# The first pair of weight chunks in two loads of 256 columns each

## The reference

```python
out_nr = _gelu(x @ w1_nr + b1_nr) @ w2_nr + b2_nr                     # condition 0
out_tsr = _gelu(x @ w1_tsr + b1_tsr) @ w2_tsr + b2_tsr                # condition 1
h = _gelu(_gelu(x @ w1_sr + b1_sr) @ w2_sr + b2_sr)                   # condition 2
out_sr = h @ w3_sr + b3_sr
y = x + out
mu, var = mean(y), mean((y - mu) ** 2)
result = (y - mu) * rsqrt(var + 1e-5) * gamma + beta
```

## Time and profile before

| | |
|---|---|
| time, median of 3 runs | 558.92 us (558.64 to 558.94) |
| the profiled execution | 559.73 us |
| its span, first to last instruction | 558.0 us |
| what lies around the span | 1.7 us |
| PE busy | 548.7 us, 98% |
| DVE busy | 270.7 us, 49% |
| ACT busy | 215.6 us, 39% |
| POOL busy | 252.1 us, 45% |
| granted clock of TensorE, mean | 0.997 |

### The profile page before, as it was taken

How to read it: one execution, slowest core, us unless ns; L and a number is a source line. 1 busy time by engine, 2 the same in 40 slices (tenths; PEclk the granted TensorE clock), 3 DMA queues, 4 the chain that set the end, 5 groups by cost and what they waited for, 6 DMA issues and landing times. The chain is left out here.

```text
span 558.0 us, 8218 instructions
## 1 busy us (share of the span) xinstructions
PE 548.7 (98%) x2416; PEld 452.2 (81%) x2417; DVE 270.7 (49%) x432; ACT 215.6 (39%) x335; POOL 252.1 (45%) x212
## 2 busy tenths in 40 slices
PE   8999999999999999999999999999999999999994
PEld 5888888888888888888888888888888888888883
DVE  5650176865856856114710568112765105501656
ACT  5451236145344354214421452424255124513353
POOL 0989997775674575300430046600174300530056
PEclk9999999999999999999999999999999999999998
DMA  8984405345344443200320044400244101310032
GB/s 303 360 265 149 152 1 196 105 151 179 113 159 143 158 152 139 87 0 0 137 89 0 5 153 143 150 0 0 75 156 157 63 0 37 141 48 0 0 135 93
DMA packets 26369, 61.26 MB, mean 110 GB/s; under 512 B 3058, under 2 KB 3314, under 8 KB 26226
## 3 DMA queue, kind: packets, MB, share of 16 engines
q1 hardware_dynamic: 26208, 60.97, 31.9%
q10 hardware_dynamic: 146, 0.13, 0.1%
HBM read 44.31 MB, written 16.78 MB: 109 GB/s over the span
## 5 line engine op out<-in xcount | busy, mean ns | idle before, releaser
L489 DVE TENSOR_TENSOR g_lo<-bank,g_hi 128x512 fp32r<-128x512 f32 x112 | 77.4, 691 | 251.5 <-DVEq L121 251.5
L421 ACT ACTIVATE g_hi<-bank,bcol 128x512 fp32r<-128x512 f32 x112 | 77.8, 695 | 166.4 <-ACTq L121 165.0
L643 POOL TENSOR_TENSOR y<-y,row 128x512 f32<-128x512 f32 x64 | 96.2, 1523 | 48.2 <-POOLq L121 47.9
L459 ACT ACTIVATE y<-y,rstd 128x512 f32<-128x512 f32 x63 | 42.4, 717 | 159.8 <-ACTq L121 159.8
L248 PE MATMUL bank<-w_hi,g_hi 128*128 128x512 f32 x256 | 99.6, 389 | 0.0
L249 PE MATMUL bank<-w_lo,g_hi 128*128 128x512 f32 x256 | 99.6, 389 | 0.0
L250 PE MATMUL bank<-w_hi,g_lo 128*128 128x512 f32 x256 | 99.6, 389 | 0.0
L248 PE MATMUL bank<-x_hi,w_hi 128*128 128x512 f32 x240 | 93.4, 389 | 0.0
L249 PE MATMUL bank<-x_lo,w_hi 128*128 128x512 f32 x240 | 93.4, 389 | 0.0
L250 PE MATMUL bank<-x_hi,w_lo 128*128 128x512 f32 x240 | 93.4, 389 | 0.0
L649 POOL TENSOR_SCALAR var_eps<-mv 128x2 f32<-128x2 f32 x15 | 3.3, 217 | 185.5 <-POOLq L121 185.4
(11 more groups left out here) (51 smaller groups left out, 597.0 us busy)
## 6 DMA issues: line engine op xcount, KB each, us to landing
y<-x SPq DMA_DIRECT2D x64, 256.0 KB, 3.6
out<-y SPq DMA_DIRECT2D x63, 256.0 KB, 2.5
stage<-x_t SPq DMA_DIRECT2D x31, 512.0 KB, 3.4
w_raw<-weights SPq DMA_DIRECT2D x17, 512.0 KB, 4.5
row<-rows SPq DMA_DIRECT2D x1, 1280.0 KB, 11.1
stage<-x_t SPq DMA_DIRECT2D x2, 256.0 KB, 3.8
w_raw<-weights SPq DMA_DIRECT2D x2, 256.0 KB, 4.9
out<-y SPq DMA_DIRECT2D x1, 128.0 KB, 1.9
```

Of the source, the lines that this page charges most:

```text
L421: eng.activation(g_hi[:, slot, :], psum, ACT.Gelu, bias=b)
L459: eng.activation(y[:, t, :], y[:, t, :], ACT.Copy, scale=rstd[:, t:t + 1]).then_inc(s_n, 1)
L489: eng.tensor_tensor(g_lo[:, slot, :], psum, g_hi32[:, slot, :], ALU.subtract).then_inc(s_gs, 1)
L643: eng.tensor_tensor(y[:, t, :], y[:, t, :], row[:, kind, :], ALU.add).then_inc(s_xb, 1)
```

## The change

The loads of weights chunks 0 and 1 are cut in two, columns 0 to 255 and 256 to 511, each with its own semaphore. A partition's row in such a load is 1 KB in place of 2 KB. DVE, which cast each chunk in two halves before, now waits ahead of each half for that half's load, where it waited once for the whole chunk. On SP the two halves of a chunk are issued one behind the other, in the chunk's old place.

```diff
-        s_w_piece = [sem(f"s_w_piece{c}") for c in range(2)]
+        s_w_piece = {(c, n): sem(f"s_w_piece{c}_{n}") for c in range(2) for n in (0, T // 2)}
...
             for c in range(2):
                 n = slice(c * T, c * T + T)
                 eng.dma_start(stage[:, 0, c, :], x_halves[0][:, n]).then_inc(s_x_piece[c], 16)
-                eng.dma_start(w_raw[:, c, :], weights[0][:, n]).then_inc(s_w_piece[c], 16)
+
+                for h in (slice(0, T // 2), slice(T // 2, T)):
+                    eng.dma_start(w_raw[:, c, h], weights[0][:, c * T + h.start:c * T + h.stop]).then_inc(s_w_piece[c, h.start], 16)
             load_x(x_halves[1], 1)
...
             for c in range(2):
-                eng.wait_ge(s_w_piece[c], 16)
                 for half in (slice(0, H // 2), slice(H // 2, H)):
+                    eng.wait_ge(s_w_piece[c, half.start], 16)
                     eng.tensor_copy(w_hi[:, c, half], w_raw[:, c, half]).then_inc(s_first_w, 1)
                 x_low(c, c + 1, (s_nr, s_x01)[c])
                 eng.wait_ge(s_first_w, 2 * c + 2)
```

## The result

The changed kernel is slower by a little: the median of 17 runs is 559.75 us (558.69 to 560.22), against 558.83 us (558.28 to 559.85) for 17 runs of the kernel before. The ratio is 1.0014, with a 95% interval of 1.0008 to 1.0021, about 0.8 us. That is clear of no change and within the 0.2% that counts as the same. The profiled execution took 559.75 us with a span of 558.0 us, so it is a usual one of the changed kernel. That of before, 559.73 us, had the same span and was 0.9 us above the median of the 17; only one of them was slower. The two traces therefore end at the same time, and are compared here for what they wait for and not for their length.

The account below looks back on a forecast made before the run. PE, busy without gaps after its start, was taken as the bound; 0.20 to 0.27 us gained at the start less 0 to 0.1 us for smaller packets, taken as 0.2 us, made 558.92 - 0.2 = 558.7 us; range 557.9 to 559.5 us.

Parts of the forecast that it names:

- The place: The change touches the start alone; what PE gains there reaches the end one for one, unless something later makes it wait.
- L: Landing time of half b of weights chunk 0, taken as unchanged at 5.92 us; x_lo 0 would end 0.92 us later.
- x_lo 0.20 to 0.27 us earlier: At the start, one cast less behind half b's landing: PE's x_lo products come 0.20 to 0.27 us earlier, near 7.15 us.
- part (1): Two more issues on SP, 0.48 us apart: later loads issued 0.95 us later, off the path while the engines have backlog.
- Rival A: At the start, the DMA hold-up doesn't come back: PE starts at 5.31 us, gain 1.0 to 1.17 us, 557.8 us; chance 0.13.
- Rival C: At the start, half b lands later and delays x_lo: 559.2 us, or 559.5 us with a later landing; chance 0.17.
- The fixed 2.0 us: Skill's fixed cost per DMA; paid in series it would put half b 2 us later, the time about 1.8 us up.
- Part (2): Smaller packets in the split loads: two of 1 KB take 90 ns against 88 for 2 KB; cost 0 to 0.1 us a chunk.
- The bound of 1.17 us on the gain: Most PE can gain at the start: 1.07 us of idling plus 0.10 us lost inside the first four products.
- the failing sign: ACT's casts from 8.53 or 9.82 us come so late that PE waits at 11.70 us: the prediction would be wrong.

Follow-up runs that it names:

- the one without the gate: Kernel before, but its first batch does chunks 0 and 1 twice in place of chunks 2 and 3 (wrong output): 558.75 us, ratio 0.9995.

## Why the prediction was wrong

- **The place was right.** Nothing but the start moved, and what PE gains or loses there reaches the end; the stretch from 28 us on is the same to 0.05 us.
- **The sum's own base was an exception.** I took L = 5.92 us as what every run has, and dismissed the rest with "the runs of before agree within 0.30 us, so what sets the landing comes every time". That was three runs. Seventeen spread over 1.57 us, the profiled one was near their top, and three traces with the first four loads issued alike show the first product at 5.24 to 5.29 us, not 6.38. (The second trace of the kernel before has 6.63 us, in an even slower execution.) I had the hint in hand: the profiled execution stood 0.8 us above the median, and I only subtracted that. The term "x_lo 0.20 to 0.27 us earlier" was the gain in such a late start, which most runs probably don't have.
- **The step that failed is part (1), the two issues on SP.** The sum made 558.7 us, and 559.75 us was measured. I wrote that "the queue ahead sets their landing and not the issue" and gave 0.4 us of cover if it slid by 0.95 us all the same. Both parts failed. The casts slid by 1.22 and 1.24 us, more than the 0.95 us of the issues. And the cover was measured against PE at 11.70 us, which holds for a start at 6.38 us alone; from a start at 5.02 us PE is there at 10.7 us, while the first cast of weights chunk 2 ended near 11.7 us: PE stood still for 0.99 us. Two effects that I had costed apart, an earlier start and later data, meet at this gate.
- **Rival A had the start nearly right and the end wrong.** It had the first product at 5.31 us and weights chunk 2 "just in time", at 10.4 against 10.6 us. But it was worked out with the data of chunk 2 at its old time, though the same change makes it later. It was the change's own gain at the start that could only be kept with that data in time.
- **Rival C named the right sign and the wrong gate.** Half b did not land late (1.70 + 3.2 = 4.9 us), and with DVE waiting for both halves the time was the same. The fixed 2.0 us of the Trainium skill ("DMA: Bandwidth & Descriptors", "Anatomy of one DMA") are given in that section for DMAs that GpSimd issues, and these come from SP. The trace shows no 2 us in series: the casts of the two halves of chunk 0 start at 4.58 us and some 0.4 us later. The Trainium skill's advice to coalesce (the same page, "Rules for kernel authors") came out right for this kernel, though not through small packets: 256 packets of 1 KB in one load cost nothing.
- **Part (2) was right**: packets of 1 KB cost nothing that can be told (0.9999, 0.9990 to 1.0008). The bound of 1.17 us on the gain counted from a warm-up that ends at 5.31 us; in the changed kernel's trace it ended at 4.95 us, and the first product came 1.36 us earlier. At the end the bound was not tested, since no kernel gained: none came under the 558.75 us of the one without the gate by more than the noise.
- **The chances** put 0.91 on "within 0.2%", where it landed, and the range ended at 559.5 us, 0.25 us too low. I had written the failing sign down myself, ACT's casts from 8.53 and 9.82 us so late that PE waits for them, as a thing that would prove me wrong, and had given it no chance.

**What is shown and what is not.** Shown: the loss is in the loads and not in DVE's waits; not in the packets' size, nor in their number; it goes when the halves b are issued from another queue, and comes without any split when one tiny load (1.0009, 1.0000 to 1.0018) or both (1.0014, 1.0005 to 1.0023) stand ahead of x chunk 1. So the changed kernel pays for the issue that half b of chunk 0 puts in front of x chunk 1 and of all that follows on SP's queue. In the traces the time is paid where PE waits for the data of chunk 2, or at a gate beside that one. Not settled: why, with chunk 0 alone split, 0.47 us of delay on SP goes with a cast of weights chunk 2 at 10.97 us instead of 9.82 us; why the same kernel has its data at such different times from run to run; and whether the second queue helps by earlier issues or in another way. What holds a packet up was not found.

## What to carry to other kernels

In a start where several loads are used one after the other, an issue put in ahead of others can cost more than its own time in all that lands behind it, so list the gates in order (first product, next chunk, next layer) and work out each with both effects at once: the engine that comes earlier and the data that comes later. When the one profiled execution lies far above the median, its start or its stalls may not be those of the usual run; look for the surplus before building on a single landing time. And where a piece must be split, the extra issue can go on another engine's queue, which here cost nothing, but gained nothing either. One trace a kernel is a sample of one: where the trace's own time stands far from its kernel's median, as in two kernels here, it is the wrong witness for that median.

## What was unexpected in the hardware

**The same loads land at very different times from run to run.** Weights chunk 0, whole and issued at 1.22 us in each, landed 4.7 us behind its issue in the earlier trace rows. It is also the shorter of two landings in the second trace of before, 4.9 us; in the kernel before without the wait ahead of chunk 2, 3.6 us; and with a tiny load behind each chunk, 3.0 us (min, median and max of the two whole chunks in each):

```profile
DMA to landing us min/median/max: 4.9/5.3/5.7
...
DMA to landing us min/median/max: 3.6/4.1/4.7
...
DMA to landing us min/median/max: 3.0/3.5/3.9
```

The four loads of halves in the changed kernel took 3.2 to 4.2 us.

**Single packets are held up, while most are not.** In the first 9 us of the trace of before, half of the 2 KB packets took 84 ns or less, and half of the 4 KB ones 159 ns or less, but 13 packets took over 500 ns, the longest 2.05 us; of the 1 KB packets in the changed kernel half took 46 ns or less. So the 152 ns a packet that the prediction found between 4 and 6 us is a mean of packets at full pace and a few that stand. The fifteen traces with SP alone have 5 to 20 such packets, the five with weights on ACT's queue too have none to 6.

**The clock of TensorE can rise late, and this costs 1.6 us.** In the second trace of before (561.61 us) the first products run slowly:

```profile
4.61 0.95 PE L380 MATMUL bank<-const-bfloat16-1.0 128*128 128x128 bf16 x7
6.63 2.05 PE L287 MATMUL bank<-x_hi,w_hi 128*128 128x512 f32 x4 [1.06 <-DVE w_hi L597]
8.47 1.80 PE L287 MATMUL bank<-x_lo,w_hi 128*128 128x512 f32 x4
10.12 1.09 PE L287 MATMUL bank<-x_hi,w_lo 128*128 128x512 f32 x4
```

Four products take 8.47 - 6.63 = 1.84 us and then 1.65 us, where the earlier trace rows has 1.01 and 0.91 us, and from 10.12 us on the rhythm is as there. The slow ones follow one another by 0.43 us, and 512 columns in 0.43 us are the lower of the two levels, 1.2 GHz. That costs 1.84 + 1.65 - 1.01 - 0.91 = 1.6 us. PE had idled 1.06 us before, as it had in the earlier trace rows without such a loss, but the two executions differ ahead of that idle time: the last seven warm-up products took 0.95 us here and 0.69 us in the earlier trace rows. The granted clock is recorded in the trace from 10.02 us on here, and from 4.87 us on in the first trace of before, while the warm-up still ran. So nothing shows a clock that fell in the idle time; in one execution it had risen before it, in the other it rose only after the first eight products. The kernel with chunk 0 split and chunk 1 by ACT (561.55 us) has a second such trace, recorded from 9.85 us on. The mean of the clock over a stretch reads 1.00 here too, because it has no record from before 10.02 us; the products' own rhythm is the better witness:

```profile
6.60:10.00 3.40, 3.37 (x8) 2.72 (x9) 3.10 (x8) 1.38 (x3) 0.00 (x0) 1.00 1.01 392
```
